# x's normalisation on GpSimd behind the deviation, V's bias and the output block's copy at other heads

## What is computed

```python
# x = layernorm(x), D = 256, H = 16 heads of 16 columns
q, k, v = x @ Wq.T + bq, x @ Wk.T + bk, x @ Wv.T + bv
scores = einsum("bihd,bjhd->bhij", q, k) / 4
logits = (x @ rel_W[:, :d].T)[:, :, None] + (x @ rel_W[:, d:].T)[:, None] + rel_b
bias = einsum("bijk,hk->bhij", softmax(logits), logical_bias)
scores = scores + sigmoid(x @ gate_W.T + gate_b) * bias
out = (softmax(scores) @ v) @ Wo.T + bo
```

## Time and profile before

| what | us |
|---|---|
| median of three runs (lowest, highest) | 6042.34 (6040.91, 6044.29) |
| the profiled execution's own time | 6042.3 |
| its span, from the first to the last instruction | 6040.5 |
| TensorE busy over the span | 5365.8 (89%) |
| VectorE busy | 4701.5 (78%) |
| ScalarE busy | 4409.7 (73%) |
| GpSimd busy | 3704.9 (61%) |

### The profile page before, as it was taken

How to read it: one execution, slowest core, us unless ns; L and a number is a source line. 1 busy time by engine, 2 the same in 40 slices (tenths; PEclk the granted TensorE clock), 3 DMA queues, 4 the chain that set the end, 5 groups by cost and what they waited for, 6 DMA issues and landing times. The chain is left out here.

```text
span 6040.5 us, 114022 instructions
## 1 busy us (share of the span) xinstructions
PE 5365.8 (89%) x40162; PEld 3532.6 (58%) x40162; DVE 4701.5 (78%) x6099; ACT 4409.7 (73%) x7005; POOL 3704.9 (61%) x2010
## 2 busy tenths in 40 slices
PE   6888888898989898888799869999999979999999
PEld 4666666666666666655344345555555546666665
DVE  6999999999999999998888679999999942122221
ACT  4999999999999999999366678888888821111111
POOL 3888888888888888875100079999999930000000
PEclk8999999999999999999899889999999989999999
DMA  2121121212112121200355555555555521111110
GB/s 74 28 49 31 28 51 28 51 28 51 28 34 45 30 48 31 46 17 14 129 190 211 187 211 187 208 208 191 195 201 207 184 101 42 45 35 35 35 35 11
DMA packets 461255, 537.80 MB, mean 89 GB/s; under 512 B 237537, under 2 KB 337761, under 8 KB 460785
## 3 DMA queue, kind: packets, MB, share of 16 engines
q1 hardware_dynamic: 460784, 531.75, 28.0%
HBM read 370.31 MB, written 161.35 MB: 88 GB/s over the span
## 5 line engine op out<-in xcount | busy, mean ns | idle before, releaser
L502 DVE CUSTOM_DVE_ANT_0 srow<-srow,ps_s,small 128x1024 f32<-128x1024 f32 x1024 | 1304.0, 1273 | 63.5 <-issue 34.6
L576 ACT ACTIVATE srow<-srow,nmax 128x1024 f32<-128x1024 f32 x1024 | 1200.0, 1172 | 87.3 <-DVE nmax L502 78.3
L585 ACT COPY AT<-ps_t 128x512 f32<-128x512 f32 x2048 | 1110.5, 604 | 19.8 <-PE ps_t L658 18.8
L658 PEld LDWEIGHTS ps_t<-ident,srow 128*128 128x128 f32 x8192 | 954.9, 141 | 224.2 <-issue 36.3
L658 PE MATMUL ps_t<-ident,srow 128*128 128x128 f32 x8192 | 1068.7, 273 | 2.8 <-ACT AT L585 2.4
L1977 POOL TENSOR_TENSOR c_hc<-c_hs,c_cs 128x1024 f32<-128x1024 f32 x432 | 1009.9, 2364 | 61.2 <-DVE c_hs L2079 59.1
L491 DVE SCALAR_TENSOR_TENSOR srow<-ps_p,rho,R 128x1024 f32<-128x1024 f32 x768 | 975.3, 1270 | 0.0
L1938 PE MATMUL c_ps_y<-c_hc,c_ident 128*128 128x512 f32 x2048 | 944.8, 594 | 29.9 <-DVE c_y L2062 21.4
L2079 DVE TENSOR_TENSOR_SCAN c_hs<-c_da,c_pd 128x1024 f32<-128x1024 f32 x384 | 860.1, 2273 | 54.6 <-PE c_pd L1929 54.6
L647 PE MATMUL ps_s<-K,Q 96*128 96x512 bf16 x2048 | 617.1, 383 | 291.2 <-DVE nmax L502 265.3
L2022 ACT ACTIVATE c_sT<-c_dxT,c_bT 128x256 f32<-128x256 f32 x1536 | 668.4, 494 | 107.0 <-PE c_pd L1929 96.9
(11 more groups left out here) (256 smaller groups left out, 8576.5 us busy)
## 6 DMA issues: line engine op xcount, KB each, us to landing
c_cs<-bc_d SPq DMA_DIRECT2D x256, 512.0 KB, 4.3
c_bs<-bc_d SPq DMA_DIRECT2D x64, 512.0 KB, 6.5
Q<-parts_d SPq DMA_DIRECT2D x384, 64.0 KB, 2.3
parts_d<-parts SPq DMA_DIRECT2D x57, 384.0 KB, 3.4
K<-parts_d SPq DMA_DIRECT2D x168, 128.0 KB, 4.4
sz_d<-b_sz SPq DMA_DIRECT2D x16, 1024.0 KB, 7.1
xv_d<-b_xv SPq DMA_DIRECT2D x16, 1024.0 KB, 7.8
dt_d<-b_ab SPq DMA_DIRECT2D x16, 1024.0 KB, 4.2
```

Of the source, the lines that this page charges most:

```text
L502: nc.vector.tensor_tensor_reduce(r[:], r[:], ps_s[:], small[:, slot, h:h + 1], BIG, ALU.add, ALU.min, nmax[:, h % NROW:h % NROW + 1]).then ...
L576: nc.scalar.activation(r[:], r[:], ACT.Exp, scale=-1.0, bias=nmax[:, h % NROW:h % NROW + 1]).then_inc(e_ok, 1)
L585: nc.scalar.copy(AT[h % NAT][:, HG * half:HG * half + HG, :], ps_t[:, half]).then_inc(at_ok, 1)
L658: last = nc.tensor.transpose(ps_t[:, half, i, :], rows_sb[h % NROW][:, j * P:(j + 1) * P], ident[:])
```

## The change

`xn` is made by GpSimd, right behind `pool_rstd`, and no longer by VectorE at u = 5; the same holds for the one xn made ahead of the loop. Since GpSimd now reads `mv`, VectorE waits for `x_free` before it writes the next `mv`. `dve_v` goes from u = 4 to u = 5. ScalarE's `act_o` goes from u = 5, ahead of `act_at`, to the end of u = 4, behind `act_at` and `act_rel` and ahead of e(5).

```diff
+        def pool_xn(pool, p, k):
+            alone(pool, rstd_ok, p + 1, pool_own)
+            nc.gpsimd.tensor_scalar(xn[:], xt[:, k, :], mv[:, 0:1], rstd[:, 0:1],
+                                    ALU.subtract, ALU.mult).then_inc(x_free, 1)
...
         def dve_ln(dve, p, k):
             wait(dve, x_in_s, 16 * p + 16)
             nc.vector.bn_stats(stats[:], xt[:, k, :]).then_inc(ln_step, 1)
+            alone(dve, x_free, p + 2, dve_own)
             alone(dve, ln_step, 3 * p + 1, dve_own)
...
-        def dve_xn(dve, p, k):
-            wait(dve, rstd_ok, p + 1)
-            nc.vector.tensor_scalar(xn[:], xt[:, k, :], mv[:, 0:1], rstd[:, 0:1],
-                                    ALU.subtract, ALU.mult).then_inc(x_free, 1)
...
                 pool_rstd(pool, NT)
+                pool_xn(pool, NT, 0)
                 pool_g_rstd(pool, 1)
...
                 if pro:
                     pool_rstd(pool, t + AHEAD)
+                    pool_xn(pool, t + AHEAD, 1 - k)
...
                     if pro and u == 5:
-                        dve_xn(dve, t + AHEAD, 1 - k)
-                    if pro and u == 4:
                         dve_v(dve, t + NT, 1 - par, ib)
...
-            dve_xn(dve, NT, 0)
             dve_g_ln(dve, 1)
...
                     act_e(act, t, u)
-                    if post and u == 5:
-                        act_o(act, t - 1)
...
                     if look and u in (1, 3, 4):
                         act_rel(act, t + 1, 1 - k, after(par, ib, 1), (1, 3, 4).index(u))
+                    if post and u == 4:
+                        act_o(act, t - 1)
```

## The result

The changed kernel takes 6056.03 us (median of 17 runs), the kernel before 6042.18 us (17 runs beside them): 1.0021 times, with a 95% interval of 1.0013 to 1.0028. I had forecast 6033.4 us and given the range 6020 to 6054; the time lies 2 us outside it, on the slow side. One of the 17 runs took 8018.41 us at a granted clock of 0.63 where all others had 0.98; it counts in the median (6055.80 without it) and not in the ratio. The profiled execution took 6053.2 us with a span of 6051.4 us.

A forecast was written before the change was run, and what follows sets the result against it. A ring of waits through ScalarE, GpSimd, VectorE and TensorE was taken to set the 43.27 us tile. Terms 56 x -0.09 = -5.0, -2.0 and -1.9 sum to -8.9 us: 6042.3 - 8.9 = 6033.4 us, range 6020 to 6054.

The forecast's parts named there:

- The ring: Chain of waits from e(2) through ScalarE, GpSimd, VectorE and TensorE to the next e(2); its 43.27 us is the tile.
- The margin ahead of `pool_t`: GpSimd's idle while `pool_t` waits for ScalarE's second logarithm step: 1.01 us by which GpSimd's work could come later.
- the one behind the second sum: Margin between the end of GpSimd's second sum and ScalarE's logarithm behind it: 0.99 us after the hand-over.
- xn on GpSimd: The moved instruction takes 0.48 us, delaying what follows on GpSimd by 0.66 us; slow bound 1.07 us, 1.25 us delay.
- the slow xn: Rival: GpSimd's xn takes 1.07 us, each tile gains 0.2 us, the kernel takes 6049.9 us; chance 0.22.
- ScalarE's 0.09 us: ScalarE's wait for TensorE's transposes at its copy of AT behind e(6) goes, shortening each tile by 0.09 us.
- VectorE's and TensorE's gain: At heads 4 to 6 VectorE gets 0.6 to 0.8 us early, TensorE 0.67; beside the ring, so worth nothing.
- The copy of O: ScalarE's 0.62 us copy, moved from u = 5 to u = 4 within the same busy stretch: 0.
- the added wait: VectorE's wait for `x_free` ahead of bn_aggr, at u = 2 behind s(2): between 0 and 0.18 us, taken as 0.
- Ahead of the loop: TensorE's first products start earlier because GpSimd makes the first xn: -1.9 us, bounds 0 and 2.2.
- The stall of 2.0 us: One tile's VectorE xn took 2.60 us beside GpSimd's L387, mean 0.64; without it -2.0 us, bounds 0 and 2.3.
- The permanent collision: Rival: `pool_rem` regularly holds VectorE's relation step 1, 56 x 0.77 = 43 us, the kernel takes 6076 us; chance 0.05.

## Why the prediction was wrong

- **What bounds the kernel: right.** The ring's links are the same after the change but for the one that GpSimd feeds, and that one's 0.34 us is the tile's. The margin ahead of `pool_t`, which I read as 1.01 us, was measured as 1.02 and 1.00 by the two shorter xn; the one behind the second sum, 0.99 us, has no run of its own.
- **xn on GpSimd: the step that failed.** "I take 0.48 us: subtract and multiply are arithmetic with pointers as in L408, while L414 has a min." It is 1.22 us. With the gap of 0.22 us that is 1.44 us against a margin of 1.0, where I had 0.66, and it made +0.35 us a tile, 19 us in all. The pair subtract and multiply goes at L414's rate, and multiply and add at L408's (0.55 us with the very same pointers). Even the upper bound of 1.07 us was too low: L414's fixed part, 1070 - 256 x 3.28 = 230 ns, is below xn's, 1224 - 840 = 384 ns. L414 has constants where xn has pointers; that this is the cause wasn't tried. The Trainium skill, "GPSIMD Engine Reference", section 3.1, has one rate for short bodies, 1.03 cycles per element at 1.2 GHz. By it an estimate is 0.22 us on top of L418's 0.28, 0.50 us. The kernel with multiply and add is near it with 0.55 us, the changed kernel with 1.22 us isn't.
- **The rival that came true** was the slow xn, with a chance of 0.22 and a threshold of 0.75 us. Its working, put through with 1.22 us for 1.07, gives 0.35 us a tile and 6042.3 + 56 x 0.35 - 3.6 = 6058.3 us; the runs gave 6056.0. That they lie so close is in part luck: up to the last `dve_y` the profiled execution lost 14.2 us where this working has 16.0, and it took 3.3 us less behind it, which nothing in my sum stands for. The mechanism and the margin were right, its price wasn't, and so the upper end of the range, 6054, was 2 us too low.
- **ScalarE's 0.09 us: too large.** Where xn is cheap the tile is 43.24 or 43.25 us, 0.02 to 0.03 less than 43.27. I took the distance of two starts, 1.14 us where its neighbour had 1.04. That distance did fall to 1.05 us, and ScalarE's second logarithm step starts 0.10 us earlier behind e(2): with 16 columns 1028.87 - 1011.24 = 17.63 us, before 1035.73 - 1018.00 = 17.73. But it takes 1.15 us there instead of 1.08, so its end, on which GpSimd waits, is only 0.03 us earlier. In that stretch the recorded durations creep up, from 1.16 us for e(4) to 1.29 us for e(10), while the next start is 1.05 us behind each. 56 x -0.02 = -1.1 us and not -5.0.

```profile
1011.24 1.15 ACT L577 ACTIVATE srow<-srow,nmax 128x1024 f32<-128x1024 f32 x1 [0.46 <-DVE nmax L503]
...
1028.87 1.15 ACT L572 ACTIVATE R<-R 128x1024 f32<-128x1024 f32 x1
```

- **VectorE's and TensorE's gain is worth nothing: right.** TensorE's wait for the copy of O fell from 0.72 to 0.41 us (I said 0.3); `dve_y` idles 0.9 us (I said 1.2). The kernel with two more reads on VectorE kept its tile to 0.02 us.
- **The copy of O and the added wait at 0: right**, the first by a run of its own, the second since the kernels with a shorter xn have that wait too, and tiles of 43.24 and 43.25 us, below the 43.27 before.
- **Ahead of the loop: about right.** From the deviation's start to TensorE's first product of xn it was 21.09 - 17.59 = 3.50 us and is 2.09 (below): -1.4 us, where I took -1.9; the slow xn is the difference. The first `dve_y` comes 2.9 us earlier in this execution, and between 1.0 and 3.4 us in the kernels with xn on GpSimd. Part of that is the start of the deviation, which the change leaves alone: it is 17.59 us before and 15.93 after, and varies between these two and 17.84 over the kernels.

```profile
15.93 0.56 POOL L368 TENSOR_TENSOR rstd<-ve,mhalf 128x1 f32<-128x1 f32 x1 [7.81 <-DVE ve L442]
16.73 1.23 POOL L372 TENSOR_SCALAR xn<-xt,mv,rstd 128x256 f32<-128x256 f32 x1 [0.23 <-POOL rstd L368]
...
18.02 0.69 PE L606 MATMUL ps_m<-ident,xn 128*128 128x128 f32 x2 [2.12 <-POOL xn L372]
```

- **The stall of 2.0 us: gone, and others in its place.** The tile with the xn of 2.60 us is a plain 43.6 now, but step 1 of the relation is long in 5 tiles instead of 3. The long tiles cost 7.8 us above the steady length after, 9.1 before: -1.3 us in all where I took -2.0.
- **The permanent collision** didn't come with this change. Its 6076 us in my text is a slip: with 43 us and the two gains of 2.0 and 1.9 it is 6081.5. Three kinds of it came in the kernels that I made (xn, `dve_y`, step 1), each with 0.9 to 1.0 us on VectorE's instruction: a shift of a few tenths of a microsecond can bring one.

## What to carry to other kernels

Price an instruction on GpSimd by a row with the same pair of operations, not by one of the same form: 0.55 and 1.22 us differ by nothing else in the instruction. Where an engine's list has a margin, compare it with the whole of what is put in, and where it doesn't do, look for work in the same list that can go elsewhere: the same xn of 1.22 us cost 0.37 us a tile in one order and nothing in another. Before moving an instruction by tenths of a microsecond, look for what the other of VectorE and GpSimd starts within the width of the move, on both sides.

## What I had not expected of the hardware

- GpSimd's tensor_scalar with subtract and multiply costs 3.28 ns a column (436, 800, 1224 ns for 16, 128, 256 columns; one kernel each); with multiply and add 256 columns take 550 ns.
- One instruction of GpSimd holds one of VectorE up to its own end. xn, 0.40 us by itself, then ends 0.15 us behind it (0.64 or 1.55 us, by when it starts); `dve_y` (2.17 us instead of 1.23) and the relation's step 1 (2.25 instead of 1.27) end 1.08 us behind it.
- Which of the two is held follows the recorded starts only up to an offset: step 1 is held up to a lead of its own of 0.040 us and not from 0.046 us on, and VectorE's xn of the earlier trace rows was held with a lead of 0.08 us. In a schedule that repeats it falls out the same way in nearly every tile; a single wait on the right side turned 55 long steps into 1.
- Moving V's bias on VectorE from ahead of xn to behind it cost 59 us in one run, with no instruction added: where an engine is held until a set time, the work ahead of the held instruction is free and the work behind it isn't.
